# A spectral tokenizer with one attention block: a shorter input ring, and eighteen groups kept on chip instead of twelve

## The reference, cut to what matters

```
coeff = jax.lax.complex(xi[..., 0], xi[..., 1]) * sqrt_eig.astype(jnp.complex64)
x = jnp.einsum('nlm,mlk->nkm', coeff, pct.astype(jnp.complex64))
u = jnp.fft.irfft(x, n=NLON, axis=-1, norm='forward')
...
h = _L0_tok_ref(x, L0_tok_sqrt_eig, L0_tok_pct, 64)
h = h + _L0_attn_ref(_layernorm(h, axis=-1), L0_attn_K, L0_attn_temperature, L0_attn_bias)
h = h + _L0_ffn_ref(_layernorm(h, axis=-1), L0_ffn_W, L0_ffn_b)
```

## Time and profile before

| | us |
|---|---|
| median of 3 runs (1432.6 to 1438.91) | 1435.57 |
| the profiled execution | 1430.64 |
| its span in the profile | 1428.6 |
| PE busy | 1334.1 (93%) |
| DVE busy | 929.4 (65%) |
| ACT busy | 899.9 (63%) |
| POOL busy | 559.5 (39%) |

### The profile page before, as it was taken

How to read it: one execution, slowest core, us unless ns; L and a number is a source line. 1 busy time by engine, 2 the same in 40 slices (tenths; PEclk the granted TensorE clock), 3 DMA queues, 4 the chain that set the end, 5 groups by cost and what they waited for, 6 DMA issues and landing times. The chain is left out here.

```text
span 1428.6 us, 30500 instructions
## 1 busy us (share of the span) xinstructions
PE 1334.1 (93%) x8813; PEld 1158.9 (81%) x8813; DVE 929.4 (65%) x2026; ACT 899.9 (63%) x1956; POOL 559.5 (39%) x1394
## 2 busy tenths in 40 slices
PE   4999778798999999999999999999999989999994
PEld 3778666588899999999999999999999989545551
DVE  1232222235777878878788887888878878767772
ACT  1223222234677777777777777777777777867772
POOL 0000000000355555555555555555555546732222
PEclk8999999999999999999999999999999999999997
DMA  8999999994653433434334343343434332100000
GB/s 346 424 425 424 425 425 425 425 376 146 192 130 92 94 79 96 86 83 90 79 98 85 82 86 82 99 83 83 85 82 100 82 93 59 50 12 9 9 4 5
DMA packets 88315, 219.69 MB, mean 154 GB/s; under 512 B 20784, under 2 KB 33724, under 8 KB 75900
## 3 DMA queue, kind: packets, MB, share of 16 engines
q1 hardware_dynamic: 78728, 190.33, 42.8%
q10 hardware_dynamic: 4164, 27.27, 4.5%
q0 software_dynamic: 5376, 1.52, 0.6%
HBM read 147.77 MB, written 72.68 MB: 154 GB/s over the span
## 5 line engine op out<-in xcount | busy, mean ns | idle before, releaser
L674 PE MATMUL ps_k<-sphi,Glo 128*128 128x256 f32 x1024 | 292.2, 285 | 0.0
L673 PE MATMUL ps_k<-splo,Ghi 128*128 128x256 f32 x1024 | 291.0, 284 | 0.0
L672 PE MATMUL ps_k<-sphi,Ghi 128*128 128x256 f32 x1024 | 288.6, 282 | 0.0
L261 PE MATMUL s1b<-pg,cg 128*128 128x256 f32 x1024 | 240.5, 393 | 48.0 <-DVE cg L231 46.8
L261 PEld LDWEIGHTS s1b<-pg,cg 128*128 128x128 f32 x1024 | 198.0, 196 | 93.0 <-issue 33.9
L231 DVE TENSOR_TENSOR cg<-xg,se 128x1024 f32<-128x1024 f32 x63 | 77.2, 1225 | 221.5 <-DMA pg<-in_pct_dram 211.0
L1442 POOL TENSOR_SCALAR ve<-var 128x2 f32<-128x2 f32 x64 | 13.9, 217 | 479.8 <-ACT squares L1049 479.7
L672 PEld LDWEIGHTS ps_k<-sphi,Ghi 128*128 128x128 f32 x1024 | 194.7, 190 | 2.4
L673 PEld LDWEIGHTS ps_k<-splo,Ghi 128*128 128x128 f32 x1024 | 193.1, 189 | 2.7
L674 PEld LDWEIGHTS ps_k<-sphi,Glo 128*128 128x128 f32 x1024 | 193.7, 189 | 0.0
L316 ACT COPY stage<-s1b 128x512 f32<-128x512 f32 x104 | 60.7, 585 | 169.5 <-PE s1b L261 165.2
(11 more groups left out here) (175 smaller groups left out, 3181.0 us busy)
## 6 DMA issues: line engine op xcount, KB each, us to landing
pg<-in_pct_dram SPq DMA_DIRECT2D x63, 1024.0 KB, 25.7
out_dram<-o SPq DMA_DIRECT2D x64, 512.0 KB, 2.8
xg<-in_xs_dram SPq DMA_DIRECT2D x63, 512.0 KB, 24.2
xt<-spec SPq DMA_DIRECT2D x60, 512.0 KB, 5.2
spec<-stage ACTq DMA_DIRECT2D x52, 512.0 KB, 8.1
rrow<-rs SPq DMA_DIRECT2D x64, 128.0 KB, 4.6
spec<-hold SPq DMA_DIRECT2D x12, 480.0 KB, 5.2
recs<-rec SPq DMA_DIRECT2D x16, 160.0 KB, 5.6
```

What stands on the lines that cost most here:

```text
L261: last = nc.tensor.matmul(bank[at * PARTS + part][:, m % 2, :], cg[:, b % SETS, m * 2 + h, :], pg[:, b, m * 2 + h, :], start=(h == 0), sto ...
L672: nc.tensor.matmul(out_ap, whi, mhi, start=(j == 0), stop=False)
L673: nc.tensor.matmul(out_ap, whi, mlo, start=False, stop=False)
L674: last = nc.tensor.matmul(out_ap, wlo, mhi, start=False, stop=(j == n - 1))
```

## The change

The ring `RING1` of stage 1 has four slots instead of eight, and 22 groups are written out instead of 20. Eighteen groups stay on chip (`KEPT`) instead of twelve: groups 46 to 51 go to a new tile `apart` of 24 KB in each of the 128 partitions, at a fixed address that overlaps parts of the later tiles `h`, `h2` and `o`; `h` is allotted later so that this is so. ScalarE reads the part of image 0 out of `apart` in groups 56 and 58. In stage 2 SyncE loads image 1 (92 rows from `spec`, and its rest from `hold` and `apart`), then stores `apart` of images 2 to 63 to `spec` in two transfers of 62 rows of 24 KB. Images 2 and 3 are loaded in slot 0 after `rrow` 0, once that store has landed; hold stores follow with two pairs in each of the slots 0, 1 and 2. VectorE waits for the store before it writes `h` of block 2. The eight small constants are loaded from ScalarE's queue, at the start of stage 1.

```diff
-RING1 = 8
+RING1 = 4
-LEAD = 20
+LEAD = 22
 HELD = 12
+APART = 6
+KEPT = HELD + APART
 FROM = P - HELD * GM // 2
+FIRST_KEPT = P - KEPT * GM // 2
+APART_AT = 196352
...
+        self.apart = nc.alloc_sbuf_tensor_at("apart", [P, APART * GM, NLAT], F32, offset=APART_AT)
...
+        def first_apart(eng, c):
+
+            eng.dma_start(const.x0[FIRST_KEPT:FROM, 2 * c:2 * c + 2, :].rearrange("p q w -> p (q w)"),
+                          const.apart[c * NB:c * NB + 1, :, :].rearrange("o (p q) w -> o p (q w)", q=2)
+                          ).then_inc(const.x0_loaded, 16)
...
             for b in range(RING1):
                 load(b, b)
                 if b == 1:
-                    for dst, src in ((Kf, K_in), (FT, FT_in), *others):
+                    for dst, src in ((Kf, K_in), (FT, FT_in)):
                         sp.dma_start(dst, src).then_inc(const_loaded, 16)
...
-            sp.dma_start(const.x0[0:FROM].rearrange("p (h q) w -> p h (q w)", h=2),
-                         spec[0].rearrange("(h p q) w -> p h (q w)", h=2, q=2)[0:FROM]).then_inc(const.x0_loaded, 16)
+            sp.dma_start(const.x0[0:FIRST_KEPT].rearrange("p (h q) w -> p h (q w)", h=2),
+                         spec[0].rearrange("(h p q) w -> p h (q w)", h=2, q=2)[0:FIRST_KEPT]
+                         ).then_inc(const.x0_loaded, 16)
...
-                held = isinstance(g, int) and g >= GROUPS - HELD
+                held = isinstance(g, int) and g >= GROUPS - KEPT
...
-                    if held:
+                    if held and g < GROUPS - HELD:
+                        at_m = (g - GROUPS + KEPT) * GM + 2 * j
+                        to = const.apart[:, at_m:at_m + 2, :]
+                    elif held:
...
+                if isinstance(g, int) and g in (GROUPS - 8, GROUPS - 6):
+                    act.wait_ge(copied, (GROUPS - HELD) * PARTS)
+                    first_apart(act, (g - GROUPS + 8) // 2)
...
+            for dst, src in others:
+                act.dma_start(dst, src).then_inc(const_loaded, 16)
             groups(nc.scalar, group)
...
-            for n in range(1, 4):
-                sp.dma_start(xt[0:FROM, n].rearrange("p (h q) w -> p h (q w)", h=2),
-                             spec[n].rearrange("(h p q) w -> p h (q w)", h=2, q=2)[0:FROM]).then_inc(x_loaded[n], 16)
+            def load_first(n, rows):
+                sp.dma_start(xt[0:rows, n].rearrange("p (h q) w -> p h (q w)", h=2),
+                             spec[n].rearrange("(h p q) w -> p h (q w)", h=2, q=2)[0:rows]).then_inc(x_loaded[n], 16)
                 for c in range(2):
                     sp.dma_start(xt[FROM:P, n, 2 * c:2 * c + 2, :].rearrange("p q w -> p (q w)"),
                                  const.hold[c * NB + n:c * NB + n + 1, :, :].rearrange("o (p q) w -> o p (q w)", q=2)
                                  ).then_inc(x_loaded[n], 16)
+
+            load_first(1, FIRST_KEPT)
+            for c in range(2):
+                sp.dma_start(xt[FIRST_KEPT:FROM, 1, 2 * c:2 * c + 2, :].rearrange("p q w -> p (q w)"),
+                             const.apart[c * NB + 1:c * NB + 2, :, :].rearrange("o (p q) w -> o p (q w)", q=2)
+                             ).then_inc(x_apart, 16)
+            m_apart = NLAT - KEPT * GM
+            for c in range(2):
+                sp.dma_start(spec[2:NB, c * NLAT + m_apart:c * NLAT + m_apart + APART * GM, :],
+                             const.apart[c * NB + 2:c * NB + NB, :, :]).then_inc(apart_stored, 16)
...
-            store_held(0, 1)
...
+                if isinstance(i, int) and i == 0:
+                    sp.wait_ge(apart_stored, 32)
+                    load_first(2, FROM)
+                    load_first(3, FROM)
                 if isinstance(i, int) and 0 <= i < 3:
-                    store_held(1 + 2 * i, min(3 + 2 * i, 6))
+                    store_held(2 * i, 2 * i + 2)
...
+                    if isinstance(n, int) and n == 2:
+                        dve.wait_ge(apart_stored, 32)
```

More of the change, by code:

```diff
@@ L88, in __init__ @@
         self.hold = sb("hold", [P, HELD * GM, NLAT])
+        self.apart_at = APART_AT
+        self.apart = nc.alloc_sbuf_tensor_at("apart", [P, APART * GM, NLAT], F32, offset=APART_AT)
     def add_ffn(self, nc, ctx):
@@ L161, in groups @@
                 group(g, g % RING1)
-            with eng.Fori(LEAD, GROUPS - HELD - RING1 + 1, RING1) as g0:
+            with eng.Fori(LEAD, GROUPS - KEPT - RING1 + 1, RING1) as g0:
                 for u in range(RING1):
                     group(g0 + u, (LEAD + u) % RING1)
-            for g in range(GROUPS - HELD, GROUPS):
+            for g in range(GROUPS - KEPT, GROUPS):
                 group(g, g % RING1)
@@ L200, in _ @@
             for half in range(2):
-                sp.wait_ge(stored[half], 32 * ((GROUPS - HELD) // 4))
-            sp.dma_start(const.x0[0:FROM].rearrange("p (h q) w -> p h (q w)", h=2),
-                         spec[0].rearrange("(h p q) w -> p h (q w)", h=2, q=2)[0:FROM]).then_inc(const.x0_loaded, 16)
+                sp.wait_ge(stored[half], 32 * ((GROUPS - KEPT + 2 - 2 * half) // 4))
+            sp.dma_start(const.x0[0:FIRST_KEPT].rearrange("p (h q) w -> p h (q w)", h=2),
+                         spec[0].rearrange("(h p q) w -> p h (q w)", h=2, q=2)[0:FIRST_KEPT]
+                         ).then_inc(const.x0_loaded, 16)
             for m0, m1 in ((0, (HELD - 2) * GM), ((HELD - 2) * GM, (HELD - 1) * GM), ((HELD - 1) * GM, HELD * GM)):
@@ L339, in _ @@
             for half in range(2):
-                act.wait_ge(stored[half], 32 * ((GROUPS - HELD) // 4))
+                act.wait_ge(stored[half], 32 * ((GROUPS - KEPT + 2 - 2 * half) // 4))
 def stage2_blocks(nc, const, ffn_consts, spec, recs, rs, out):
@@ L388, in stage2_blocks @@
         y = place("y", held_at + 45568, [P, 512])
-        h = sb("h", [P, 4, TILES, NLON])
         hhi = sb("hhi", [P, 2, TILES, NLON], F32R)
@@ L401, in stage2_blocks @@
         pTlo = sb("pTlo", [P, TILES, NLAT], F32R)
+        h = sb("h", [P, 4, TILES, NLON])
         h2 = sb("h2", [P, 2, TILES, NLON])
         o = sb("o", [P, 2, TILES, NLON])
+        assert nc.sbuf_base <= APART_AT + APART * GM * NLAT * 4 + 31
         x2 = sb("x2", [P, 2, TILES, P])
@@ L454, in stage2_blocks @@
         x_loaded = [sem(f"x_loaded{i}") for i in range(4)]
+        x_apart = sem("x_apart")
+        apart_stored = sem("apart_stored")
         rs_written = sem("rs_written")
@@ L539, in wait_spectrum @@
             if isinstance(n, int) and n == 0:
-                eng.wait_ge(const.x0_loaded, 16 * 7)
+                eng.wait_ge(const.x0_loaded, 16 * 9)
+            elif isinstance(n, int) and n == 1:
+                eng.wait_ge(x_apart, 32)
+                eng.wait_ge(x_loaded[1], 48)
             elif k == 0:
```

## The result

| | median | runs |
|---|---|---|
| before | 1435.19 us | 1432.60 to 1438.91, 4 runs |
| after | 1490.60 us | 1484.30 to 1496.29, 4 runs |
| ratio | 1.0383 | 95% interval 1.0327 to 1.0438 |

The change makes the kernel 55 us slower; 1484.9 (1436 to 1503) was forecast.

What follows compares the result with a forecast made beforehand. Stage 1 was taken as bound by bytes, stage 2 by TensorE, its first blocks by the `rs` round trip; -9.0 + 50.9 + 4.2 + 3.2 = +49.3 us on 1435.57 gives 1484.9 us, range 1436 to 1503.

Steps and rivals of the forecast that it cites:

- Two engines: Store at stage 2's opening: engines are the largest divisor of the row count up to 16, so 62 rows use two.
- the two readings: Image loads and hold stores: rows dealt evenly over 16 engines, or engines equal to the row count's largest divisor up to 16.
- The length of the store: Opening of stage 2: 1.524 MB per engine at 26.3 GB/s takes 57.9 us, delaying `rrow` 0; +50.9 us (50 to 67).
- Blocks 1 and 3: Early stage 2: image loads behind `rrow` 0 cost +4.2 us (0 to 6), extra hold stores in slot 2 +3.2 (0 to 4).
- Stage 1: All of stage 1 together, from fewer stores, earlier constants and the shorter ring: -9.0 us (-7 to -11).
- The opening: Start of stage 1: small constants off SyncE's queue bring group 3 summed 2.9 us earlier (0 to 4.5).
- The ring: Stage 1, four slots: group 22 lands 2.4 us after 19 is summed, 1.2 us given back; the queue does not run dry.
- the six groups: Stage 1: six groups fewer stored, three pairs at 2.43 us each, 7.3 us less.
- At nothing: Terms put at zero: TensorE's lower clock after idling, two small ScalarE reads late in stage 1, block 0's 92-row load.
- B (an even deal): Store rows go over all engines; passage terms 9.8 against -9.0, +0.8 us, 1436.4; chance 0.14.
- C (a hidden passage): Even deal at 425 GB/s, the two later terms worth 1 us together; -7.7 us, 1427.9; chance 0.07.
- D (a starving ring): Stage 1 queue runs dry after group 22; one us short per group is +41 on B, 1477; chance 0.05.

Runs made afterwards that it cites:

- rows61: Changed kernel with the six-group store split into row 2 alone and rows 3 to 63 (61 rows); 1536.54 us, single execution.
- rows64_8k: The changed kernel with the store over all 64 rows, each half in three transfers of 8 KB rows; 1437.22 us, one execution.
- ring4_only: The kernel before with a ring of four groups and nothing else changed; ratio to before 1.0016 (0.9999 to 1.0033).
- rows64: Changed kernel with the six-group store over all 64 rows of each half; 1436.03 us, ratio to before 1.0044 (1.0026 to 1.0062).
- early_store: Changed kernel, 64-row store issued by ScalarE late in stage 1, images 2 and 3 loaded ahead of `rs` 0; 1435.34 us, ratio to before 1.0008.
- late_store: Changed kernel, 64-row store behind `rrow` 0, images 2 and 3 reading six-group rows on chip, hold stores redealt; 1445.32 us, ratio to before 1.0065.

## Why the prediction was right, and where its sizes were off

**Two engines.** Right, and shown by five row counts. It was read off two rows, 0.85 and 0.78, where the 60-row stores could not tell the two readings apart.

**The length of the store.** The step of the largest error: +61.5 where I put +50.9. In the trace's records of single rows the store begins at 323.1 (my 330.5, less the 8.3 us of stage 1, is 322.2) and ends at 392.9: 69.8 us for 1.524 MB an engine, 21.8 GB/s, where I had 57.9 us. I had taken 26.3, from the stores of stage 1, over 21.1, from the nearest stretch of this same queue, on the argument that long rows have less overhead. The average lies at the value I did not take, but the rate was not constant:

```profile
340.00:350.00 10.00, 0.00 (x0) 0.00 (x0) 0.00 (x0) 0.00 (x0) 0.00 (x0) 0.54 0.13 37
360.00:370.00 10.00, 0.00 (x0) 0.00 (x0) 0.00 (x0) 0.00 (x0) 0.00 (x0) 0.50 0.12 52
380.00:390.00 10.00, 0.00 (x0) 0.00 (x0) 0.00 (x0) 0.00 (x0) 0.00 (x0) 0.50 0.13 54
```

From 360 us on the two engines moved 26 to 27 GB/s each, the rate I had taken, and the one engine of `rows61` does so from 330 us on (27 GB/s). Before 360 us they moved 17 to 21 (33, 37 and 42 GB/s for the two). What failed is the assumption of one rate for the whole store; what slowed its first 40 us stays open, and on sixteen engines `rows64_8k` showed no effect of the rows' length. Three smaller differences come beside it: `rrow` was issued 0.5 us after the store's end and not 3.1, the store began 0.9 us later than I had it, and `lsc` 0 followed `rrow`'s issue in 3.6 us, not 3.2.

**Blocks 1 and 3.** +2.0 for 4.2 and +2.4 for 3.2. The loads of images 2 and 3 take 4.6 us of SyncE's queue behind `rrow` 0 (393.77 to 398.34), and `rs` 1 is issued 6.4 us behind `lsc` 0, 3.6 us more than before (346.57 less 343.76). Its way to `rrow` 1 was shorter, 5.7 us (403.41 to 409.15) where before took 7.5 (346.57 to 354.07), and that gave 1.8 us back. I had taken this way to keep its length.

**Stage 1, -8.3 for -9.0.** The sum is close, but its terms were each too small and cancelled, so that it came out so well is in part luck. The opening brought more: the first side product starts at 35.18, 5.05 us sooner, not 2.9, since group 2's load is issued at 5.21 instead of 12.60. SyncE's queue:

```profile
5.21 0.43 SPq L189 DMA_DIRECT2D xg<-in_xs_dram  x1
```

The ring took more. TensorE's stretch, and VectorE's groups 21, 22 and 62 and the last half:

```profile
35.18 3.60 PE L285 MATMUL s1b<-hold 128*128 128x512 f32 x8
...
110.99 13.98 PE L274 MATMUL s1b<-pg,cg 128*128 128x256 f32 x64
```

```profile
119.92 1.23 DVE L244 TENSOR_TENSOR cg<-xg,se 128x1024 f32<-128x1024 f32 x1 [4.62 <-DMA pg<-in_pct_dram]
124.77 1.22 DVE L244 TENSOR_TENSOR cg<-xg,se 128x1024 f32<-128x1024 f32 x1 [3.63 <-DMA pg<-in_pct_dram]
...
306.20 1.23 DVE L244 TENSOR_TENSOR cg<-xg,se 128x1024 f32<-128x1024 f32 x1 [2.43 <-DMA pg<-in_pct_dram]
...
310.00 0.69 DVE L241 TENSOR_TENSOR cg<-xg,se 128x512 f32<-128x512 f32 x1 [1.17 <-DMA pg<-in_pct_dram]
```

Group 19 is summed at 118.06 (110.99 + 7.07), group 22 scaled 6.7 us later; I had said 2.4. The load of 22 was issued where I put it (114.81, 3.25 us ahead), but it took 10.0 us to be scaled and not 5.7. I had given it the engines to itself; it shares them with the load of 21, issued at 107.92 and scaled 12.0 us later, and with the stores of two groups. So at group 22 nothing is left of the opening (124.77 against 124.32), and `ring4_only` shows nearly the same, 6.1 us. From there the six groups bring 8.5 us by group 62 (181.4 us for 189.9) and 1.0 more in the last halves, where I had 7.3 in all; 0.8 is lost again between the last half and the first issue of stage 2 (7.0 us for 6.2).

**At nothing.** The return from the lower clock was in fact covered: `lsc` 1 waited for `rrow` all the same. For the small reads by ScalarE no wait of their own was found in the trace.

**The rivals.** B (an even deal) is refuted by the row counts; and its price was too low, as `rows64`, which has all 16 engines, is +13.0 us in the passage and not +9.8. C (a hidden passage) is refuted by `rows64`, `early_store` and `late_store`. D (a starving ring) is refuted by the share of 1.02 from 130 to 300 us, and `ring4_only` has 1.02 as well (150 to 290 us).

## What to carry to other kernels

Before a transfer is cut to "the rows that are needed", look at the largest divisor up to 16 of its row count: two useless rows more (64 for 62) are worth some 50 us here (52.6 to `lsc` 0; 48 by the ratios to before, 1.0383 and 1.0044), and a single 1 KB write behind the odd transfer pays for all of it. Bytes taken off a bound stage have to go somewhere: here three places for the same 3 MB were tried (ahead of `rs` 0, behind it, at the end of stage 1 from another queue), and each held up something small, so that a gain of 8 us never reached the end. Look for the first thing that waits for a transfer at the new place, and ask of a rate whether it was measured on the same tile and on as many engines: the same queue, direction and row length gave 311 GB/s for `hold` and 210 for `apart` here.

## What the runs showed of the hardware

- The rate of one engine differs with how many take part, for the same rows of 24 KB written to `spec`: 26.4 GB/s with one (2.70 MB in 6.4% of 16 engines in 100 us), 22.1 with two on average (2.14 MB in 12.1% of 16 engines in 50 us), 22.7 with nine, 16.6 with fifteen, 14.1 with sixteen. In total the last three are 201, 222 and 205 GB/s, while this core's traffic in stage 1, loads and stores mixed, is 425. So nine engines are as good as sixteen for this store. What limits it was not found; the stores of `hold`, with the same direction and distance between rows, made 311. Whether it is the tile's place in SBUF, the place in `spec` or the number of rows was not tried.
- `rs`, 1 KB, behind the store on one engine, blocked SyncE itself in `rows61`: its issue took 48.89 us, so nothing else could be issued either.

```profile
326.69 48.89 SPq L667 DMA_DIRECT2D rs<-rstd  x1
```

- TensorE's clock fell within a short idle too: in `rows64` TensorE is empty from about 337.8 to 347 us, and the granted clock is 0.73 in 340 to 345 and 0.50 in 345 to 350.
